# Eight attention batches written out in a row instead of a loop over five of them, and the inputs of a batch loaded two batches ahead

## The reference, cut to what matters

```python
sup = relu(ctx @ W_fc.T + b_fc);  ref = relu(layernorm(x) @ W_fc.T + b_fc)
q = ref @ W_q.T + b_q;            k = sup @ W_k.T + b_k
p = softmax(q k^T / 4, per head); attn = (p @ sup) @ W_v per head + b_v
x = x + ref + attn
x = x + experts(layernorm(x), top 2 of 8) + base(layernorm(x))
```

## Time and profile before

| what | us |
|---|---|
| median of 3 runs | 1425.2 |
| lowest and highest run | 1423.08, 1428.62 |
| the profiled execution | 1423.38 |
| its span | 1421.6 |
| last L460 of the attention starts at | 992.6 |
| granted TensorE clock over the span, mean | 0.953 |

### The profile page before, as it was taken

How to read it: one execution, slowest core, us unless ns; L and a number is a source line. 1 busy time by engine, 2 the same in 40 slices (tenths; PEclk the granted TensorE clock), 3 DMA queues, 4 the chain that set the end, 5 groups by cost and what they waited for, 6 DMA issues and landing times. The chain is left out here.

```text
span 1421.6 us, 24901 instructions
## 1 busy us (share of the span) xinstructions
PE 1277.0 (90%) x8100; PEld 885.3 (62%) x8101; DVE 742.6 (52%) x1550; ACT 679.5 (48%) x938; POOL 240.9 (17%) x236
## 2 busy tenths in 40 slices
PE   4779997997999799799979979999959999999992
PEld 4647775775777577577757757755525556666661
DVE  4246675675667566566756746777435112111113
ACT  4326664664756566466656646665622112222220
POOL 3311110211111111121111102000013601222110
PEclk9879999998999999899989989999979999999996
DMA  4663454455444446444444644453079501111115
GB/s 142 200 174 94 131 138 108 106 154 125 131 117 123 116 114 159 115 131 129 100 116 121 173 112 113 108 106 62 13 222 280 221 26 45 44 44 44 48 45 189
DMA packets 154927, 168.56 MB, mean 119 GB/s; under 512 B 69040, under 2 KB 140344, under 8 KB 154816
## 3 DMA queue, kind: packets, MB, share of 16 engines
q1 hardware_dynamic: 151360, 157.61, 42.1%
q0 software_dynamic: 3456, 9.47, 1.8%
HBM read 103.55 MB, written 63.31 MB: 117 GB/s over the span
## 5 line engine op out<-in xcount | busy, mean ns | idle before, releaser
L602 DVE TENSOR_REDUCE mx<-side 128x1 f32<-128x400 f32 (+1 forms) x1024 | 534.6, 568 | 142.6 <-PE side L454 130.6
L497 ACT ACTIVATE prob<-st 128x1024 f32<-128x1024 f32 (+1 forms) x416 | 411.6, 1022 | 215.8 <-PE st L475 215.4
L454 PE MATMUL side<-kst,qst 96*128 96x400 f32 (+1 forms) x1024 | 330.1, 382 | 3.8 <-DVE mx L602 2.4
L475 PE MATMUL st<-qst,kst 97*128 97x512 f32 (+1 forms) x832 | 268.8, 406 | 35.3 <-issue 28.8
L454 PEld LDWEIGHTS side<-kst,qst 96*128 96x128 f32 x1024 | 189.8, 190 | 115.6 <-issue 37.4
L487 PE MATMUL acc<-prob,v 128*32 128x256 f32 (+1 forms) x3328 | 207.6, 385 | 0.0
L475 PEld LDWEIGHTS st<-qst,kst 97*128 97x128 f32 (+1 forms) x832 | 149.3, 188 | 49.9 <-issue 32.1
L634 POOL TENSOR_TENSOR clo<-raw,chi 128x768 fp32r<-128x768 f32 (+1 forms) x32 | 60.8, 1900 | 517.3 <-ACT chi L528 517.3
L487 PEld LDWEIGHTS acc<-prob,v 128*32 128x32 f32 (+1 forms) x3328 | 95.7, 110 | 79.6 <-issue 23.3
L1432 DVE TENSOR_TENSOR hg<-sg,pu 128x512 f32<-128x512 f32 x40 | 27.5, 688 | 138.4 <-PE pu L1610 138.4
L640 POOL TENSOR_TENSOR flo<-fc,fhi 128x768 fp32r<-128x768 f32 (+1 forms) x32 | 61.0, 1907 | 217.0 <-ACT fhi L541 217.0
(11 more groups left out here) (162 smaller groups left out, 1431.9 us busy)
## 6 DMA issues: line engine op xcount, KB each, us to landing
kst<-parts_at SPq DMA_DIRECT2D x90, 400.2 KB, 5.5
parts_at<-parts SPq DMA_DIRECT2D x48, 384.0 KB, 5.1
v<-v_at SPq DMA_DIRECT2D x32, 408.0 KB
raw<-ctx_t SPq DMA_DIRECT2D x24, 384.0 KB, 3.3
v_at<-vst SPq DMA_DIRECT2D x32, 272.0 KB
wall<-gate_up SPq DMA_DIRECT2D x8, 1024.0 KB, 14.1
parts_at<-parts SPq DMA_DIRECT2D x16, 449.0 KB, 2.8
qst<-q_at SPq DMA_DIRECT2D x192, 32.0 KB, 5.8
```

Source lines behind the costliest of these rows:

```text
L454: pe.matmul(side[u.bank][:, 0:w], t.qst[0:96, pair, col * P:(col + 1) * P], t.kst[0:96, pair, o:o + w], start=True, stop=True).then_inc(si ...
L475: mm = pe.matmul(into[0:rows, i * 2 * NQ:(i + 1) * 2 * NQ], t.kst[0:97, GP * g + i, s * P:s * P + rows], t.qst[0:97, GP * g + i, :], start ...
L497: act.activation(prob[0:rows, s, :], st[(KT * g + s) % 2][0:rows, :], ACT.Exp, scale=float(DH) ** -0.5).then_inc(exp_done, 1)
L602: dve.tensor_reduce(mx[:, hq, r:r + 1], side[u.bank][:, 0:RANGES[r][1]], AX.X, ALU.max)\
```

## The change

The loop is gone: `batches` writes out all eight bodies with constant addresses and counts. The load of the input of batch 1 moves into the part ahead of batch 0. The load for batch b + 2 stands in the third group of batch b, where it waits for `dve_resid_x` of the second group of the same batch.

```diff
@@ -738,11 +738,7 @@
         def batches(eng, body):
-
-            body(0, 0)
-            with eng.Fori(1, LOOP_TO) as b:
-                body(b, 1)
-            for b in range(LOOP_TO, B):
+            for b in range(B):
                 body(b, b)
@@ -784,6 +780,7 @@
                     if c == len(CHUNKS) - 1:
                         sp_load_values(sp, 0, 0)
+                sp_load_x(sp, 1, before_unit(("xres", 0, 0)))
                 sp_max_row(sp, before_unit(("tm", 0, 0)), 0)
@@ -794,8 +791,8 @@
                         if last + 1 < PHASES:
                             sp_load_values(sp, *behind(b, g, 1))
-                        if g == 0 and at + 1 < B:
-                            sp_load_x(sp, b + 1, resid_unit(b, at))
+                        if g == 2 and at + 2 < B:
+                            sp_load_x(sp, b + 2, body_unit(b, at, 1, "xres", 0))
```

## The result

The kernel with both changes takes 1351.7 us (median of 4 runs, 1351.2 to 1355.1) against 1426.9 us before (4 runs); the ratio is 0.948, with a 95% interval of 0.9451 to 0.9509. Forecast were 1355 us and a range of 1349 to 1376. The profiled execution's span is 1353.4 us, 68.2 less than before. The medians differ by 75.2. The changed kernel's profiled execution is the slowest of its four (1355.13 us), while the one before (1423.38) is 0.3 us above the fastest run of that kernel; what follows accounts for the 68.2 of the two profiles, and where the other 7 us lie stays open.

A forecast was written before the change was run, and what follows sets the result against it. TensorE, busy 90% of the span, was taken to set the pace in the attention. Idle time of 55.7 us plus 13.2 of low clock, 68.9 off 1423.4, gave 1354.5; adjusted to the median, 1355 us, range 1349 to 1376.

The forecast's parts named there:

- The two waits lie over each other: At a jump back, TensorE's issue and input waits end within 2.5 us; only both changes together give the time back.
- Step 1: TensorE's idle time that goes: 28.8 us at four jumps and 26.9 for seven inputs, 55.7 us.
- step 4: VectorE does the two normalising instructions (0.73 us) at once, in the gap before the first key projection; effect 0.
- Step 2: TensorE's low clock after stops goes: 2.2 us in batches 1 to 6, 13.2; batch 0 nothing, at most 2 us.
- reference stretch: First group without a stop, from maxima transpose to second pair of input transposes, sized from batch 0's fourth group: 8.96 us.
- Step 3: SyncE's moved input loads cost 0, covered by about 5 us of idle queue; otherwise 8 us at most.
- Step 5: Dropping the loop's register arithmetic saves 0.03 us a phase, so 0; fetching straight code shows no cost.
- The cause of the stop: At a jump back, about 7 us is code fetched by DMA, with the DMA engines 94.2% busy.
- small new wait: Rival: a new wait of 1 to 3 us at each of seven batches, 1362 to 1376 us; chance 0.10.
- issue time that survives: Rival: the issue time is not the jump's and survives the writing out, 1395 us; chance 0.05.
- load that is not early: Rival: SyncE holds the moved input load back, or the stop moves to the input, 1415 to 1425 us; chance 0.02.
- late straight code: Rival: written-out code arrives late, about 7.2 us a block plus 2.2 of low clock, up to 1486 us; chance 0.02.

The follow-up runs named there:

- e1: Against the kernel with both changes: batches still written out, but the input's load left in the first group; 1422.8 us, ratio to before 0.997.
- e2: Against the kernel with both changes: the loop kept, the input still loaded early, in the third group two batches ahead; 1394.0 us, ratio 0.9777.
- e4: Against e2: in every first group, keys and queries are loaded behind the key stores instead of at the jump; 1380.7 us, ratio 0.9674.
- e6: Against e4: the first group's values are loaded behind the key stores as well; 1376.2 us, ratio 0.9644, on another chip.
- e5: Against e2: the loop covers batches 1 and 2 only, so one jump in place of four; 1366.1 us, ratio 0.9566.
- e3: Against e1: the input's load stays in the first group but goes ahead of the keys', queries' and values' loads; 1356.5 us, ratio 0.9505.
- e7: Against the kernel with both changes: input loaded in the first group, between its three key and six query loads; 1407.2 us, ratio 0.9860.

## Why the prediction was right, point by point

**The two waits lie over each other**: shown from both sides. Removing one returned its time to the other (e1: 26.9 to 55.5 us), and four stops stayed without the other (e2).

**Step 1, idle time of 55.7 us**: right, but for 1.4 us that came back as six waits of 0.2 us. I had put VectorE's part (step 4) at nothing, "at once, in the gap". It is not at once: in program order it comes behind the eight score maxima that end the fourth group of the batch before. Too small to be measured here.

**Step 2, low clock of 13.2 us**: right in the sum. For batches 1 to 6 the first groups lost 59.6 us and the idle time net of the new waits was 46.4 (55.7 less 7.95 of batch 0 less 1.4), which leaves 13.2. The reference stretch was a little short (9.50 us came out against 8.96), mostly the new wait and its gap. Over the whole first group, batches 1 and 2 lost 1.4 and 2.7 us beside their idle time and the four behind them 1.6 to 2.7. That the mean of two batches over a short stretch gave the right sum for six is in part luck. Batch 0, to which I gave nothing, lost 9.8 us for an idle time of 7.95: the clock, low on entry as the earlier trace rows have it, rose sooner: the matmuls of L419 fall from 0.52 to 0.34 us at 102.6 us now, and were still at 0.52 at 110.5 before. That is the other 1.9 us, within my upper bound of 2.

**The total**: the sum of 68.9 us is that of the two profiles, 68.2, but by parts that offset each other: 1.9 us more from batch 0 and 0.5 from the last phases, 1.4 less for the new waits and 1.6 less outside of the batches. By the medians the change gave 75.2 us against the 70 of the forecast, and no step of the sum has those 5 us. The upper end of 1364 us for the forecast alone does not follow from its reason either: half of the clock term, 6.6 us, added to 1355 is 1362.

**Step 3, the moved loads**: right. The issue took 0.81 us at 154.79 and the key stores behind it start at 159.88.

**Step 5, register arithmetic and straight code**: right for the phases' lengths. Code blocks of 16 KB per batch fell to 6 or 7 on the instruction queue q8.

**The cause of the stop**: the fetch of code, and the traces show it. In each of the 17 stops at a jump (four each before and in e2, e4 and e6, one in e5) exactly one block of 16 KB moves on q8, and TensorE restarts 1.6 to 1.8 us after it has ended. What the loads change is when the block begins: 0.3 to 0.4 us into the stop in e6, 1.4 to 1.5 in e4, 3.2 to 4.8 before and in e2, 5.0 in e5. The queues in the stop of batch 2 in e6 (323.6 to 326.9 us), then in e2 from its start at 325.8 to 330.4 us, where no code moves, and from there to its end at 333.5 (the share adds the time of all packets and can pass 100%):

```profile
q8 instruction: 1, 0.02, 2.3%
q14 instruction: 1, 0.01, 0.6%
```

```profile
q1 hardware_dynamic: 227, 1.03, 101.5%
```

```profile
q1 hardware_dynamic: 1774, 0.58, 115.3%
q8 instruction: 1, 0.02, 2.6%
q14 instruction: 1, 0.01, 1.2%
```

The statement of the Trainium skill in "Runtime: NRT & Kernel Launch", Instruction fetch mechanics, that a taken branch out of the buffered code waits for a DMA of its target, agrees with these stops (3.0 us at the least, 7.9 at the most). The 108 ns of the Trainium skill's "Advanced Engine Details and Errata", Control Flow Timing, are not what a jump costs in a body of this size. That the stop had to do with the load on the DMA engines was argued in the prediction and is shown now, but as only a little over half of it: I had read 94% load beside a stop of 7 us as the whole reason.

The feed-forward part has a hardware loop too, with seven jumps and a body of four short rounds. Its longest "issue" wait, in the waits of the changed kernel behind 1020 us, is the row below, so a jump is not dear wherever it stands. That this is a matter of the body's length is my reading of the same statement of the Trainium skill, by which only a target outside the buffered code is waited for; no run here varies the body, so it is not shown.

```profile
PEld py L1584 <- issue: 21.7, 79, 1.1
```

**The rivals**: the small new wait came, at about a tenth of its forecast size (0.2 us in six batches, where 1 to 3 in seven were feared). The issue time that survives, the load that is not early and the late straight code did not appear.

## What to carry to other kernels

Where two stops end within a few microseconds of each other, price them together: here one change alone gave 0.3%, the other 2.2% and both 5.2%. Look at what stands ahead of a small load in its queue before moving it earlier; here, putting it ahead of the eleven loads of its own group did as well as loading it two groups earlier (e3). A loop with a long body (here a batch, nine blocks of code) can pay at every jump, here 10 us with the low clock that follows, and that on two engines at least at once, so data that is in time does not help; large loads issued right at the jump more than doubled the stop (3.1 to 7.3 us).

## What I had not expected of the hardware

A jump with idle DMA engines still stops TensorE for 3.0 to 3.3 us (e6).

The low clock after a stop costs about as much after a short stop as after a long one. Taken as the length of a first group over 29.1 us, less the idle time above 0.2 us, it was 1.5 to 2.7 us in the four batches of e6 with a stop of 3.0 to 3.3 us, 2.3 in batch 1 of e7 with one of 5.0, and 1.4 and 2.7 in batches 1 and 2 of the kernel before, with 8.3 and 7.7. Over all stops of 3.0 to 8.4 us in batches 1 to 6 of all profiles it was 1.2 to 2.7. Shortening a stop from 8 to 3 us saved its idle time and little else here; removing it gave the clock back. No run has a stop between 0.4 and 3 us there.
